# One instruction over both score banks in the layers' softmax, in place of one per bank

## What is computed

```python
sim = jnp.einsum('bhwie,bhwje->bhwij', bq, bk2) * QK_SCALE
sim = jnp.where(mask, -jnp.finfo(sim.dtype).max, sim)
attn = jax.nn.softmax(sim, -1)
out = jnp.einsum('bhwij,bhwje->bhwie', attn, bv2)
...
for i in range(DEPTH):          # DEPTH = 6
    x = attn_layer(shift_tokens(x), Wqkv[i], q_scale[i], k_scale[i], Wo[i]) + x
    x = ffn_layer(shift_tokens(x), ln_g[i], ln_b[i], W1[i], b1[i], W2[i], b2[i]) + x
```

## Time and profile before

| | us |
|---|---|
| median of 3 runs | 5073.4 |
| the runs | 5070.67 to 5076.66 |
| span of the profiled execution | 5070.2 |

### The profile page before, as it was taken

How to read it: one execution, slowest core, us unless ns; L and a number is a source line. 1 busy time by engine, 2 the same in 40 slices (tenths; PEclk the granted TensorE clock), 3 DMA queues, 4 the chain that set the end, 5 groups by cost and what they waited for, 6 DMA issues and landing times. The chain is left out here.

```text
span 5070.2 us, 182187 instructions
## 1 busy us (share of the span) xinstructions
PE 4363.6 (86%) x69459; PEld 3053.5 (60%) x69459; DVE 3369.4 (66%) x7024; ACT 2462.3 (49%) x5161; POOL 2562.9 (51%) x4541
## 2 busy tenths in 40 slices
PE   8999956866899988998789988899888998799986
PEld 5777733654566655666566665666656666466663
DVE  3555533266777757777577775777757776677765
ACT  3555543222555535555355553555535555355542
POOL 0000000011787717877177872778627776278761
PEclk9999967988999999999999998999999999999998
DMA  1000001201222212222122221222212222122211
GB/s 37 5 4 4 2 1 40 70 7 41 71 65 68 57 30 66 65 65 57 37 61 65 67 53 39 65 65 65 50 39 65 65 65 50 45 61 66 65 47 34
DMA packets 453969, 243.92 MB, mean 48 GB/s; under 512 B 41158, under 2 KB 447892, under 8 KB 452116
## 3 DMA queue, kind: packets, MB, share of 16 engines
q1 hardware_dynamic: 453140, 232.66, 18.6%
HBM read 35.40 MB, written 4.19 MB: 8 GB/s over the span
## 5 line engine op out<-in xcount | busy, mean ns | idle before, releaser
L2453 DVE TENSOR_TENSOR n_tt<-n_pp,n_rot 128x1024 f32<-128x1024 f32 x768 | 922.4, 1221 | 528.9 <-ACT n_sq L2316 528.1
L1949 POOL TENSOR_TENSOR n_pre<-n_tt 128x512 f32<-128x512 f32 x768 | 961.2, 1275 | 233.1 <-DVE n_tt L2453 232.4
L2065 PE MATMUL n_pp<-n_wqkv,n_xT 128*128 128x512 f32 x1536 | 793.9, 619 | 11.1 <-ACT n_xT L2311 10.1
L1984 POOL TENSOR_TENSOR n_pre<-n_pre,n_rn 128x512 f32<-128x512 f32 x768 | 776.9, 1043 | 34.5 <-POOL n_rn L1972 34.5
L2316 ACT ACTIVATE n_sq<-n_pp 128x512 f32<-128x512 f32 x768 | 459.0, 598 | 594.0 <-PE n_pp L2065 583.4
L2081 PE MATMUL n_pp<-ident,n_pre 128*128 128x128 f32 x3072 | 452.8, 282 | 152.8 <-POOL n_pre L1984 152.6
L2328 ACT COPY n_qkT<-n_pp 128x512 f32<-128x512 f32 x768 | 437.3, 594 | 290.1 <-PE n_pp L2081 288.7
L2081 PEld LDWEIGHTS n_pp<-ident,n_pre 128*128 128x128 f32 x3072 | 366.3, 146 | 292.9 <-issue 287.8
L2460 DVE TENSOR_REDUCE n_ss<-n_sq 128x8 f32<-128x512 f32 x768 | 519.3, 676 | 0.0
L2095 PE MATMUL n_pp<-n_wo,n_OT 128*128 128x128 f32 x3072 | 403.4, 286 | 57.5 <-ACT n_OT L2334 57.5
L2095 PEld LDWEIGHTS n_pp<-n_wo,n_OT 128*128 128x128 f32 x3072 | 366.6, 196 | 102.1 <-ACT n_OT L2334 101.4
(11 more groups left out here) (263 smaller groups left out, 8187.8 us busy)
## 6 DMA issues: line engine op xcount, KB each, us to landing
n_V<-n_Vn SPq DMA_DIRECT2D x768, 128.0 KB, 2.6
n_Vx<-n_Vn SPq DMA_DIRECT2D x384, 128.0 KB, 2.5
n_Vx<-n_Vn SPq DMA_DIRECT2D x576, 64.0 KB, 2.2
n_wqkv<-in_L_ffn_Wqkv SPq DMA_DIRECT2D x6, 1536.0 KB, 6.8
e_w<-in_L_ffn_w SPq DMA_DIRECT2D x32, 256.0 KB, 3.0
m_Y<-e_ye SPq DMA_DIRECT2D x64, 64.0 KB, 2.0
n_wo<-in_L_ffn_Wo SPq DMA_DIRECT2D x6, 512.0 KB, 7.3
a_xs<-in_L_attn_x SPq DMA_DIRECT2D x16, 128.0 KB, 2.1
```

The lines of the kernel that those rows point to most:

```text
L1949: nc.gpsimd.tensor_tensor(d, s[0], s[1][:, :, ::-1, :], ALU.add).then_inc(s_add, 1)
L1984: nc.gpsimd.tensor_tensor(d, d, bcast(rn[:, j, t, 8 * half:8 * half + 8], 2, D), ALU.mult).then_inc(s_kn, 1)
L2065: nc.tensor.matmul(pp[:, c % 2, :], xT[:, j * P:(j + 1) * P], wqkv[:, t * I + 512 * half:t * I + 512 * half + 512], start=True, stop=True) ...
L2453: nc.vector.tensor_tensor(tt[:, c % 4, :, :].rearrange("p s (h d) -> p s h d", d=D), bcast(pp[:, c % 2, :].rearrange("p (h d) -> p h d", d ...
```

## The change

Maximum, subtraction, exponential and sum are each made by one instruction over both banks (1024 numbers in each of 128 partitions) in place of two of 512. Each of the semaphores that count them goes up once for each half-step instead of twice, and who waits for them counts by that.

```diff
             def masks(N, j):
-                after(pe, s_sub, 4 * N + 2 * j)
+                after(pe, s_sub, 2 * N + j)
...
             def turn_weights(N, j):
                 for e in range(2):
                     after(pe, s_On, 4 * N + 2 * j)
-                    after(pe, s_E, 4 * N + 2 * j + e + 1)
+                    after(pe, s_E, 2 * N + j + 1)
...
-            def exps(N, j, e):
-                after(act, s_sub, 4 * N + 2 * j + e + 1)
-                nc.scalar.activation(E[:, e, :], E[:, e, :], ACT.Exp).then_inc(s_E, 1)
+            def exps(N, j):
+                after(act, s_sub, 2 * N + j + 1)
+                nc.scalar.activation(E[:, :, :], E[:, :, :], ACT.Exp).then_inc(s_E, 1)
...
             def maxima(N, j):
                 after(dve, s_S, 4 * N + 2 * j + 2)
-                for e in range(2):
-                    nc.vector.tensor_reduce(nm[:, j, e, :], pS[:, e, :].rearrange("p (i s) -> p i s", s=2 * W),
-                                            AX.X, ALU.max).then_inc(s_max, 1)
+                both = pS[:, :, :].rearrange("p e (i s) -> p (e i) s", s=2 * W)
+                peak = nm[:, j, :, :].rearrange("p e i -> p (e i)")
+                nc.vector.tensor_reduce(peak, both, AX.X, ALU.max).then_inc(s_max, 1)
                 after(dve, s_ETp, 4 * N + 2 * j)
-                for e in range(2):
-                    after(dve, s_max, 4 * N + 2 * j + e + 1)
-                    nc.vector.tensor_tensor(E[:, e, :].rearrange("p (i s) -> p i s", s=2 * W),
-                                            pS[:, e, :].rearrange("p (i s) -> p i s", s=2 * W),
-                                            bcast(nm[:, j, e, :], 2, 2 * W), ALU.subtract).then_inc(s_sub, 1)
+                after(dve, s_max, 2 * N + j + 1)
+                nc.vector.tensor_tensor(E[:, :, :].rearrange("p e (i s) -> p (e i) s", s=2 * W), both,
+                                        bcast(peak, 2, 2 * W), ALU.subtract).then_inc(s_sub, 1)
...
             def sum_exps(N, j):
-                for e in range(2):
-                    after(dve, s_E, 4 * N + 2 * j + e + 1)
-                    nc.vector.tensor_reduce(rs[:, j, e, :], E[:, e, :].rearrange("p (i s) -> p i s", s=2 * W),
-                                            AX.X, ALU.add).then_inc(s_rs, 1)
-                after(dve, s_rs, 4 * N + 2 * j + 2)
+                after(dve, s_E, 2 * N + j + 1)
+                nc.vector.tensor_reduce(rs[:, j, :, :].rearrange("p e i -> p (e i)"),
+                                        E[:, :, :].rearrange("p e (i s) -> p (e i) s", s=2 * W),
+                                        AX.X, ALU.add).then_inc(s_rs, 1)
+                after(dve, s_rs, 2 * N + j + 1)
```

More of the change, by code:

```diff
@@ L2375, in attention @@
                         copy_output(N - 1, 3, bank("o", 3, -1))
-                    exps(N, j, 0)
-                    exps(N, j, 1)
+                    exps(N, j)
                     if nxt or not j:
```

## The result

The changed kernel takes 5086.0 us in the median, the kernel before 5073.3 in the runs beside it: a ratio of 1.0025 [1.0018, 1.0032], 12.7 us more. Run a second time later it gave 5079.2 against 5072.4, 1.0017 [1.0008, 1.0026], 6.9 us more. One of the sixteen runs of the changed kernel took 8217 us, at a granted TensorE clock of 0.527 where the others have 0.944 to 0.948, and the ratio leaves it out. A ratio here isn't the quotient of the two medians and differs from it by up to 0.0007: by its ratio the second result is a loss of 8.6 us. The forecast was 5077, with a range of 5069 to 5088: the time lies inside, the sign is the forecast's, and the loss is two to four times the 3.3 us that were summed up. The first interval lies almost wholly beyond the bound of 0.2%, the second on both sides of it.

What follows compares the result with a forecast made beforehand. The prediction took a chain going round between engines, not the softmax, to bound the kernel. Half-steps with small margins (0.5 us) and layers' ends (2.8) summed to 3.3 us on 5073.4, rounded to 5077 us, range 5069 to 5088.

Steps and rivals of the forecast that it cites:

- the bound of 0.2%: Whole kernel: differences within 0.2%, 10 us, were to count as no change; chance of same 0.75.
- the ring: Chain round PE, ACT, DVE and POOL that sets the time; the softmax touches it only at PE's transposes of E (L2127).
- the half-steps counted as safe: 138 of 192 half-steps, with 0.86 us or more between ACT's exponentials and L2127; no PE idle time expected there.
- The rule of the Trainium skill: Fixed instruction costs would save some 77 us by grouping; its second half, for unsaturated engines, speaks against the change.
- The steady term: L2127 in half-steps with small margins: a later E delays PE by 0.01 to 0.02 us each, 0.5 us in all.
- 32 half-steps: Those with 0.43 to 0.45 us between the end of ACT's exponentials and the start of L2127.
- the 48 half-steps: Those with a margin under 0.71 us before L2127, eight in each layer.
- its upper bound in the text, 5 us: Small-margin half-steps: if PE takes its whole 0.1 us lead for loading weights after a wait, 5 us.
- The layers' ends: Last half-step of each of six layers, no margin: L2127 starts 0.46 us later, 2.8 us in all.
- The stop in L2140: PE's 2.09 us stop at a layer's end for no shown wait; might swallow the delay there, but the whole was taken.
- an exponential as long as two of today's: Rival: exponential of 1024 takes 1.26 us, E comes 0.61 later, 12.5 us lost, 5086; chance 0.14.
- The rival on moved stops: PE's program grows by register instructions, so its stops may fall elsewhere, faster or slower; 12 us won if six went; chance 0.08.

Runs made afterwards that it cites:

- the split kernel with the change's counts: Softmax split as in the kernel before, but semaphores counted once per half-step, so PE's program is that of the change; 5093.0 us against 5079.7, ratio 1.0024.
- the two kernels with the old counts: Exponential alone joined (ratios 1.0025 and 1.0030), and all four joined (1.0032), both with PE's program as in the kernel before.

## Why the prediction was right or wrong

**The place was right.** The softmax isn't on the ring, joining DVE's three by itself wins nothing (0.9996), and lateness costs by the start of L2127. A loss comes with the joined exponential, with or without DVE's joined.

**DVE and ACT: right.** 1.22 us and 1.06, the subtraction's end where it was (2.48 us after the maximum's start, for 2.47), no more wait in the half-steps counted as safe. The rule of the Trainium skill (Perfetto Trace Analysis, Optimizing Scalar/DVE Operations) that was weighed came out by its second half, that where engines aren't saturated breaking up instructions may let work finish sooner; the trace agrees: with DVE at 66% and ACT at 48%, the joined exponential ended 0.43 us later than the split pair.

**The steady term was mis-sized.** The prediction took 0.01 to 0.02 us for each of 32 half-steps, 0.5 in all. E came 0.43 later, not 0.41, and PE passed the wait in 0.05, not 0.04; L2127 started 0.05 later in the median of the 48 half-steps, not 32, which makes about 2 us. The bodies of the change's two profiles are 9.2 and 3.5 us longer than before, 3.5 and 2.3 when POOL's longer work in them is taken off, if all of that counts. So the term is 2 to 4 us. A difference of two numbers that agree to 0.03 was given as if it were known to 0.01; its upper bound in the text, 5 us, held. (One of the 138 half-steps counted as safe had 0.80 us and not 0.86 or more, and the stop within L2140 lasted 2.36 us in four of the six layers; nothing hangs on either.)

**The layers' ends: right.** L2127 starts 0.49 us later in four of the six ends of the first profile (1.21 in the other two) and 0.48 in the mean of the second, for 0.46 predicted: 2.9 us for six. In the other two PE was at its lower clock ahead of L2127 (L2095 took 3.07 and 2.96 us for 2.05, at granted clocks of 0.62 and 0.61). The stop in L2140 doesn't swallow it.

**The step that failed** is the sum as a measure of the change: 0.5 + 2.8 = 3.3 us. Its first term was four times too small or more, and 2 to 4 and 2.9 make 5 to 7 us. That agrees with the second result, 6.9 us by the medians and 8.6 by the ratio; the first has 12.7, and its interval begins at 9, so that some of it has no place in the sum. The two profiles of the change differ in the layers' ends (184.1 us in the mean in the first, 181.6 in the second, 182.3 before), and there in the granted clock, which the prediction didn't look at; but that is one execution against another, and the first result is a median of fifteen.

**The range held in part by luck.** Its upper part, to 5088, was there for an exponential as long as two of today's, 1.26 us, and that took 1.06. The forecast's own range, 5072 to 5082, holds the second result and not the first, and "nothing that can be told from no change", within 0.2%, did not come true in the first.

**The text on PE's program was wrong**: it runs 90 instructions fewer, not more. The rival on moved stops had more in it than the 0.08 that it was given: with 63 waits ahead of the layers a stop came to stand before L2127 in all six, which cost most of 11 us. In the change itself no such stop is to be seen.

**What stays open.** The cause is shown for lateness at L2127, and for the stops with 63 waits. What the first result of the change loses beyond 5 to 7 us isn't settled, nor is the loss of the split kernel with the change's counts, where E is on time and no new stop stands before L2127. Whether PE's program makes the clock fall more at the layers' ends isn't settled either. The intervals are 0.1% to either side, 5 us.

No version beat the kernel before. Joining DVE's three and leaving the exponential split is as good as it, and no better.

## What to carry to other kernels

Before two instructions are joined, look for the margin of whoever reads their result: the split pair is a pipeline (the first half's exponential ran under the second half's subtraction), and joining it moves the whole of the later stage behind the whole of the earlier one. Look at when the first part is ready for its reader, and not only at when the whole is complete. Price the join by the consumer's margin and count the places where it is small; where lateness and margin are equal to a few hundredths, treat the term as unknown, and multiply it by its count before calling it nothing. And compare kernels that differ by 0.2% over several profiles: one execution differs from the next of the same program by as much. An edit that moves an engine's program can move its stops: a control with nothing changed but the place (63 passed waits) lost as much here as the change.

## What was not expected of the hardware

- Where the matmul itself carries the wait (the change's PE program), it starts 0.05 us after ACT's end; where a semaphore instruction of its own stands ahead (PE's program of before, exponential joined), 0.14 us. That is a part of why the two kernels with the old counts waited 3.8 and 7.5 us before L2127, and the change only 1.3.
- The end of a layer, with the same instructions in the same program and execution, took 181.2 us at a mean granted clock of 0.93 and 185.6 at 0.91.
- 63 passed waits on PE, executed once ahead of the layers, put a stop of 1.38 to 1.93 us for no named wait into L2088 at the end of every layer, where PE had run through before.
- POOL's instructions are slower by up to 0.7% in seven of the fourteen profiles (L1966 286 for 284 ns, 2568 for 2563 us busy in all), whatever the kernel; in the layers' bodies that is 5 us of POOL's time.
